# Expert stage of a four-stage block: normalisation and routing inside it, biases and closing norm batch by batch

## What is computed

```
x = layernorm(x + attention(x))              # 16 heads of 64, causal, rotary
# expert stage, 16 experts, 512 hidden, top 4
dist2  = sum((x - keys)**2, -1)
logits = -dist2 + x @ rw.T + rb              # per token 16 values
topv, topi = top_k(logits, 4); w = softmax(topv)
hidden = gelu(x @ w1[e].T + b1[e])           # all 16 experts, all tokens
out[e] = hidden @ w2[e].T + b2[e]
x = layernorm(x + sum_k w[k] * out[topi[k]])
# then 16-head attention over 4 batches, and two layers of local attention with a gated MLP
```

## Time and profile before

| | |
|---|---|
| time of three executions | median 1795.65 us (1795.16 to 1800.93) |
| the profiled execution | 1793.86 us, span 1792.0 us, mean granted PE clock 0.94 |
| PE busy | 1565.2 us, 87% of the span |
| DVE busy | 1209.4 us, 67% |
| ACT busy | 1096.4 us, 61% |
| POOL busy | 533.5 us, 30% |
| up projections, line 937 | 780 matmuls, 191.9 us |
| down projections, line 967 | 768 matmuls, 189.1 us |
| expert stage | 496.67 us to 898.19 us of the span |

### The profile page before, as it was taken

How to read it: one execution, slowest core, us unless ns; L and a number is a source line. 1 busy time by engine, 2 the same in 40 slices (tenths; PEclk the granted TensorE clock), 3 DMA queues, 4 the chain that set the end, 5 groups by cost and what they waited for, 6 DMA issues and landing times. The chain is left out here.

```text
span 1792.0 us, 31754 instructions
## 1 busy us (share of the span) xinstructions
PE 1565.2 (87%) x10386; PEld 1060.9 (59%) x10386; DVE 1209.4 (67%) x2313; ACT 1096.4 (61%) x2369; POOL 533.5 (30%) x479
## 2 busy tenths in 40 slices
PE   6999999999769999999888888858888786898875
PEld 4777777777548888888632323325555553656543
DVE  2676676676457777777666766747878646788744
ACT  2555555555258888888546666636776634767641
POOL 1222222232122222222100000027666504666621
PEclk9999999999669999999878988988999998999988
DMA  7000000000012122221000000000000000000000
GB/s 218 1 2 1 0 0 0 0 0 1 0 50 71 70 70 71 75 75 60 0 0 1 1 0 1 1 1 1 1 1 0 0 1 1 1 2 0 0 0 24
DMA packets 18812, 36.05 MB, mean 20 GB/s; under 512 B 5606, under 2 KB 10850, under 8 KB 16546
## 3 DMA queue, kind: packets, MB, share of 16 engines
q1 hardware_dynamic: 18738, 35.08, 5.8%
HBM read 33.90 MB, written 1.18 MB: 20 GB/s over the span
## 5 line engine op out<-in xcount | busy, mean ns | idle before, releaser
L873 DVE TENSOR_TENSOR m_hidp<-m_hid,m_hidp 128x512 fp32r<-128x512 f32 x260 | 182.1, 725 | 81.8 <-ACT m_hidp L832 81.6
L389 ACT ACTIVATE a_prob<-ps,a_negmax 128x512 f32<-128x512 f32 (+3 forms) x256 | 133.8, 525 | 143.8 <-DVE a_negmax L460 143.8
L837 ACT ACTIVATE m_hid<-ps,pre_w 128x512 f32<-128x512 f32 x260 | 176.9, 685 | 51.5 <-PE ps L937 51.4
L937 PE MATMUL ps<-m_xp,m_w1p 128*128 128x512 f32 x780 | 191.9, 396 | 8.1 <-DVE m_xp L865 7.2
L967 PE MATMUL ps<-m_hidp,m_w2p 128*128 128x512 f32 x768 | 189.1, 394 | 0.0
L1140 ACT ACTIVATE c_sb_pT<-ps 128x1024 f32<-128x1024 f32 x128 | 130.3, 1024 | 89.9 <-PE ps L1321 88.6
L1605 ACT ACTIVATE l_sb_prob<-ps,l_sb_negmax,l_sb_rn 128x192 f32<-128x192 f32 (+1 forms) x256 | 123.9, 494 | 92.1 <-DVE l_sb_negmax L1702 92.0
L344 POOL TENSOR_TENSOR a_qk_r<-a_qk_c,a_qk_s 128x512 f32<-128x512 f32 x64 | 81.5, 1273 | 331.0 <-DVE a_qk_s L451 331.0
L1198 DVE TENSOR_REDUCE c_sb_negmax<-ps 128x2 f32<-128x1024 f32 x128 | 153.8, 1220 | 38.7 <-PE ps L1305 38.2
L937 PEld LDWEIGHTS ps<-m_xp,m_w1p 128*128 128x128 f32 x780 | 148.8, 191 | 41.5 <-DVE m_xp L865 7.3
L967 PEld LDWEIGHTS ps<-m_hidp,m_w2p 128*128 128x128 f32 x768 | 144.1, 188 | 33.7
(11 more groups left out here) (227 smaller groups left out, 3360.9 us busy)
## 6 DMA issues: line engine op xcount, KB each, us to landing
m_gate_all<-m_gates_d SPq DMA_DIRECT2D x16, 1024.0 KB, 4.6
pre_w<-w1T SPq DMA_DIRECT2D x14, 258.0 KB, 2.7
pre_w<-w2T SPq DMA_DIRECT2D x14, 256.0 KB, 2.8
pre_wqkv<-wqkv SPq DMA_DIRECT2D x2, 768.0 KB
keep_xT<-xT SPq DMA_DIRECT2D x1, 1024.0 KB, 6.9
keep_x<-x SPq DMA_DIRECT2D x1, 1024.0 KB
out<-keep_x SPq DMA_DIRECT2D x4, 256.0 KB
pre_m_w<-l_w SPq DMA_DIRECT2D x2, 341.0 KB
```

The lines of the kernel that those rows point to most:

```text
L389: nc.scalar.activation(prob[:, u % 4, 0:width(p)], score_ps(b, p, j)[:, 0:width(p)], ACT.Exp, bias=negmax[:, u:u + 1], accum_out=den[:, b ...
L837: nc.scalar.activation(hid[:, c % 2, f, :], ps[:, f, :], ACT.Gelu, bias=w1[:, k, FF + f:FF + f + 1]).then_inc(gelu_done, 1)
L873: nc.vector.tensor_tensor(hidp[:, c % 2, 1, f, :], hid[:, c % 2, f, :], hidp[:, c % 2, 0, f, :], ALU.subtract).then_inc(low_done, 1)
L937: ins = nc.tensor.matmul(ps[:, f, :], w1p[:, k, a, f * P:(f + 1) * P], xp[:, b, c, :], start=(i == 0), stop=(i == 2))
```

## The change

- `attention0` ends with its last addition to x. Its `Norm`, the router and the logits are gone from it; keysT, rwT and rb are loaded with the later stages' constants, rb to all partitions.
- `experts0` begins with the normalisation, batch by batch. DVE takes the moments, POOL makes 1/sqrt(var + eps) and also -mean/sqrt(var + eps), ACT normalises with scale and bias, PE transposes into banks 4, 5, 6 and 4, ACT copies both to xT and to the high part xp, DVE makes the low part from PSUM. PE routes each batch with four matmuls; DVE adds the bias (a 128x16 tile, made with one matmul of ones and keys squared) when it takes the logits, and finds the maxima per batch.
- POOL's split of the first weights stands between the batches.
- The exp of the gates is issued before the GELUs of step 0. PE does up(1) before the gates' transposes, which use banks 6 and 7.
- Steps 0 to 7 and 56 to 63 are written out, the loop has 6 pairs. The b2 matmul of batch c follows the down projection of step c, its addition follows on DVE.
- No up projection, GELU or low part is made for a step 64.
- In the last expert the closing work of each batch (back transposition, copy, moments, 1/sqrt, normalising, transposition, copy) stands one to two steps behind its last gating, in the lists of all engines.

The core of the diff:

```diff
 # POOL
+        def deviation(i, b):
+            pool.wait_ge(mv_done, r + 1)
+            nc.gpsimd.tensor_tensor(var[:, i, t], mv[:, i, t, 1], eps[:, :], ALU.add).then_inc(norm_step, 1)
+            if i == 0:
+                nc.gpsimd.tensor_tensor(nmean[:, t], mv[:, 0, t, 0], neg_one[:, :], ALU.mult).then_inc(norm_step, 1)
...
+            nc.gpsimd.tensor_tensor(rstd[:, i, t], var[:, i, t], neg_half[:, :], ALU.pow).then_inc(rstd_done, 1)
+            if i == 0:
+                nc.gpsimd.tensor_tensor(nbias[:, t], nmean[:, t], rstd[:, 0, t], ALU.mult).then_inc(rstd_done, 1)
...
+        deviation(0, 0)
+        deviation(0, 1)
+        split_up(0, 0)
+        deviation(0, 2)
+        deviation(0, 3)
+        split_down(0, 0)
+        split_up(1, 1)
+        split_down(1, 1)
 # ACT
+        def normalise(b):
+            act.wait_ge(rstd_done, 2 * (b + 1))
+            for t in range(b * TPB, (b + 1) * TPB):
+                ins = nc.scalar.activation(x[:, t, :], x[:, t, :], ACT.Identity, scale=rstd[:, 0, t:t + 1],
+                                           bias=nbias[:, t:t + 1])
...
+        normalise(0)
+        normalise(1)
+        copy_xT(0)
+        normalise(2)
+        copy_xT(1)
+        normalise(3)
+        copy_xT(2)
+        copy_xT(3)
+        act.wait_ge(top_sub, 1)
+        nc.scalar.activation(tope[:, :, :], tops[:, :, :], ACT.Exp).then_inc(top_exp, 1)
         gelus(0, 0, 0)
...
+        def step(n, e, k, c, last):
+            if not (last and c == NB - 1):
+                gelus(n + 1, (c + 1) % NB, (k + (c + 1) // NB) % 2)
+            if last and c >= 1:
+                copy_x(c - 1)
+            if last and c >= 2:
+                copy_fin(c - 2)
 # DVE
+        def take_logits(b):
...
+            nc.vector.tensor_tensor(logits[:, tiles(b), :],
+                                    ps[:, b, 0:TPB * NE].rearrange("p (t e) -> p t e", e=NE),
+                                    rbias[:, None, :].broadcast_to([P, TPB, NE]), ALU.add).then_inc(lg_ev, 1)
...
+            nc.vector.tensor_tensor(xT[:, c, :], xT[:, c, :], gated[:, c % 2, :], ALU.add
+                                    ).then_inc(acc_done, 1)
+            if isinstance(n, int) and n < NB:
+
+                dve.wait_ge(b2_mm, c + 1)
+                dve.wait_ge(acc_done, NB + n + 1)
+                nc.vector.tensor_tensor(xT[:, c, :], ps[:, 6 + c % 2, :], xT[:, c, :], ALU.add).then_inc(b2_add, 1)
+            if last and c >= 2:
+                finish_norm(c - 2)
+            if last and c >= 1:
+                second_moments(c - 1)
+
+        each_step(dve, step)
+        finish_norm(NB - 2)
+        second_moments(NB - 1)
+        finish_norm(NB - 1)
 # PE
+        turn(0)
+        turn(1)
+        route(0)
+        turn(2)
+        route(1)
+        turn(3)
+        route(2)
+        route(3)
+        pe.wait_ge(w_split, 2)
+        pe.wait_ge(x_low, 1)
         up(0, 0, 0)
...
+        def step(n, e, k, c, last):
+            if not (last and c == NB - 1):
...
+                    up(n + 1, c + 1, k)
+            if at(n, 0):
+                pe.wait_ge(x_low, NB)
+                pe.wait_ge(gate_step, 7)
+                for b in range(NB):
+                    turn_gates(b)
...
+            ins.then_inc(down_mm, 1)
+            if isinstance(n, int) and n < NB:
+                bias_down(c)
+            if last and c >= 1:
+                turn_x(c - 1)
+            if last and c >= 2:
+                turn_fin(c - 2)
+
+        each_step(pe, step)
+        turn_x(NB - 1)
+        turn_fin(NB - 2)
+        turn_fin(NB - 1)
```

More of the change, by code:

```diff
@@ L274, in attention0 @@
     y_add = sem("y_add")
-    lg_mm = sem("lg_mm")
-    lg_ev = sem("lg_ev")
     NWEIGHTS = 10
-    NLATER = 5
+    NLATER = 3
     NI = NP0 * NB
     SCALE = HD0 ** -0.5
-    norm = Norm(nc, ctx, keep, ps, [0, 1, 2, 3], y_add, [NI - NB + b + 1 for b in range(NB)], "an_")
     block = ctx.enter_context(nc.Block())
@@ L522, in _ @@
         add_y(NI - 1, NB - 1)
[L525 to L532, removed]
     @block.tensor
@@ L677, in _ @@
         output(NI - 1)
[L678 to L690, removed]
 def experts0(nc, ctx, io, keep):
@@ L762, in experts0, with tiles, each_step, pair_of @@
     acc_done = sem("acc_done")
+    fin_norm = sem("fin_norm")
+    fin_mm = sem("fin_mm")
+    fin_ev = sem("fin_ev")
     STEPS = NE * NB
-    norm = Norm(nc, ctx, keep, ps, [0, 1, 2, 3], x_ev, [1, 2, 3, 4], "mn_")
+    TURN = [4, 5, 6, 4]
     block = ctx.enter_context(nc.Block())
+    def tiles(b):
+        return slice(b * TPB, (b + 1) * TPB)
+    def each_step(eng, step):
+        def pair_of(pair, last):
+            for k in range(2):
+                for c in range(NB):
+                    step(pair * (2 * NB) + (k * NB + c), pair * 2 + k, k, c, last and k == 1)
+        pair_of(0, False)
+        with eng.Fori(1, NE // 2 - 1) as pair:
+            pair_of(pair, False)
+        pair_of(NE // 2 - 1, True)
+    def at(n, k):
+        return isinstance(n, int) and n == k
     @block.sync
@@ L942, in _ @@
+        pe.wait_ge(consts, 4)
+        pe.wait_ge(route_step, 1)
+        nc.tensor.matmul(ps[:, 7, 0:NE], ones[:, :], keys_sq[:, :], start=True, stop=True
+                         ).then_inc(sq_mm, 1)
+        turn(0)
[6 more added lines that the diff above has]
+        route(3)
         pe.wait_ge(w_split, 2)
+        pe.wait_ge(x_low, 1)
         up(0, 0, 0)
-        pe.wait_ge(gate_step, 8)
-        for b in range(NB):
-            for t in range(TPB):
-                ins = nc.tensor.transpose(ps[0:NE, 4 + b, t * P:(t + 1) * P], gates[:, b * TPB + t, :], ident[:, :])
-            ins.then_inc(gT_mm, 1)
@@ L981, in _, with step @@
-        norm.tensor(pe)
+        def step(n, e, k, c, last):
+            if not (last and c == NB - 1):
+                if c == NB - 1:
+                    pe.wait_ge(w_split, 4 * (e + 1) + 2)
+                    up(n + 1, 0, 1 - k)
+                else:
+                    if at(e, 0):
+                        pe.wait_ge(x_low, c + 2)
+                    up(n + 1, c + 1, k)
+            if at(n, 0):
+                pe.wait_ge(x_low, NB)
+                pe.wait_ge(gate_step, 7)
+                for b in range(NB):
+                    turn_gates(b)
+            if c == 0:
+                pe.wait_ge(w_split, 4 * (e + 1))
+            pe.wait_ge(low_done, (n + 1) * FB + 2 * FB)
+            pe.wait_ge(mul_done, n + 1)
+            for f in range(FB):
+                for i, (a, b) in enumerate(passes):
+                    ins = nc.tensor.matmul(ps[:, 4 + c % 2, :], w2p[:, k, a, f, :], hidp[:, c % 2, b, f, :],
+                                           start=(f == 0 and i == 0), stop=(f == FB - 1 and i == 2))
+            ins.then_inc(down_mm, 1)
[5 more added lines that the diff above has]
+                turn_fin(c - 2)
```

284 lines of the change are left out of this document (179 added, 105 removed).

## The result

The changed kernel takes 1767.64 us (median of 4; 1762.30 to 1777.12), the kernel before beside it 1796.09. The profiled execution took 1764.99 us, its span is 1763.0, mean granted clock 0.949.

The account below looks back on a forecast made before the run. TensorE was taken to bound the expert loop, with gains reachable only around it: opening 23.9 less biases 3.4 gives 20.5, plus end 5.9, is 26.4 us. Forecast 1768.5 us, range 1761 to 1779.

Parts of the forecast that it names:

- The likeliest case: Whole kernel: the forecast of 1768.5 us, own range 1764 to 1774, given a chance of 0.64.
- Opening, 25.3 less 1.4 for the clock: Start of expert stage: down(0) starts 25.3 us earlier, less 1.4 for its lower clock, so 23.9 gained.
- sooner: Rival: clock stays up through turn_fin and down(0), normalising costs its lower bound; 1763 us, chance 0.08.
- Matmuls of the bias row, 8.5: Routing: 16 matmuls adding the bias row, 0.53 us each, are gone, 8.5 us in all.
- up(1) hidden, 4.2: Opening: up(1) runs on TensorE while VectorE forms the gates, so it is hidden, worth 4.2 us.
- Exp ahead of the GELUs: Opening, ScalarE: exp issued during the index search needs no table load; one load of 1.28 us leaves the path.
- Second biases, 3.4: First four loop steps: four bias matmuls cost 0.85 us each, 3.4 together, bounds 3.4 and 6.8.
- The loop body itself is the same.: Expert loop: body unchanged, so no change in its cost was reckoned beyond the second biases.
- Gate rows: First gating waits 4 us for gate rows, hidden by a hair; rival, landing 4 us later: 1772, chance 0.09.
- The end, 5.9: End of expert stage: spare up projection gone and closing work by batch save 5.9 us, bounds 4 and 8.
- only moved: Rival: batches don't overlap routing and up(1) isn't hidden, only deleted work saves, 11.5 us; 1784, chance 0.05.
- Slower loop: Rival: each up projection waits for its GELU, every one of 60 steps grows; 1805 at 0.6 us, chance 0.04.

Follow-up runs that it names:

- after_again: The changed kernel run once more, unaltered; 1768.6 us, ratio 0.9840 to the kernel before.
- i_best: Changed kernel with waiting closing transposes behind the last down projection, loop tiles at before's addresses, first w1 split behind all four batches' deviations; 1765.7 us.
- f_rank1: Changed kernel with 16 rank-1 matmuls (row of ones by row of zeros) put back into the routing; 1774.5 us, ratio 0.9851 to before.
- d_late_up: Changed kernel with up(1) put back behind the gates' transposes on TensorE; 1771.4 us, ratio 0.9856 to before.
- e_late_exp: Changed kernel with the exp put back behind the GELUs of step 0 on ScalarE; 1778.3 us, ratio 0.9867 to before.
- a_written_out: Kernel before with pairs 0 and 7 written out and nothing made for step 64; 1794.2 us, ratio 0.9984 to before.
- h_addresses: Changed kernel, same instructions, with the loop's tiles at the SBUF addresses of before; 1764.2 us, ratio 0.9802 to before.
- b_again: Repeat of a_written_out plus the second biases moved to steps 0 to 3, old opening and closing; 1789.5 us, ratio 0.9955 to before.
- c_closing_by_batch: b_again's kernel plus the closing normalisation batch by batch, so the changed kernel with before's opening; 1793.7 us.

## Why the prediction came out right

The sum was 26.4 and the stage gave 29.4 and 27.9 (S of after and after_again, against before's). The likeliest case held; its terms did less well than their sum. That the time came within 0.9 us of the forecast is partly luck: the opening gained 4.8 more than reckoned and the end 2.6 or 1.0, the biases cost 1.6 more and the loop 2.7 that were not reckoned at all.

- **Opening, 25.3 less 1.4 for the clock.** Measured 28.8, less 0.1 for a down(0) of 3.03 and not 2.94: 28.7, so 4.8 off. The steps in order: first batch ready on POOL as said (4.8 us behind the start of the last add_y, predicted 5.0); the normalising instruction 0.41 a tile for 0.37; POOL's split between the batches, which was reckoned in, held ScalarE 0.95 back, and i_best shows it was on the path. Then the routing: 0.43 a matmul and not the 0.53 read from the mixed rows, route(2) and route(3) together 3.4 and not 4.2. up(0) starts 18.4 us behind the add_y, for 20.8 predicted. The remaining error is the clock: since up(0) and up(1) run until just before the transposes, TensorE idles 0.56 us there (1.39 in after_again) and eight transposes take 1.03, all sixteen with their pause 2.4 for the 3.6 taken from before, and down(0) takes 3.03 and not 4.6. That is one half of the rival "sooner" (0.08), the clock: it stayed up in the opening in both profiles, and through turn_fin(0) and down(63) in one of them. Its other half, a cheaper normalising instruction, did not come: 0.41 is above the 0.37.
- **Matmuls of the bias row, 8.5.** f_rank1: 10.2, of which 9.1 on the path. Right in kind, mis-sized.
- **up(1) hidden, 4.2.** d_late_up: 3.7.
- **Exp ahead of the GELUs.** Counted as one load of 1.28 off the path. e_late_exp shows 5.8, some 1.0 of it by `hit`'s new place, since the whole chain behind the sum and the clock hang on it. The load itself: 1.28, and what follows starts 1.30 after its start, in after once and in e_late_exp twice. The Trainium skill (ScalarE: Activation LUTs, What ACT_TABLE_LOAD costs) gives 2.66 for a switch with its drain; no drain shows in these traces, where the same three loads start 0.01 to 0.02 behind the end of the instruction before them.
- **Second biases, 3.4.** Measured 5.0, inside the bounds (3.4 to 6.8). Halving the price with the clock was right for bias matmuls in a row: twice 0.43 in a_written_out at clock 1.00. What failed was to carry it into the loop. There the next up projection starts 1.05 behind the bias matmul's start and not 0.86, and the rounded matmuls before and after take 0.09 longer each: 1.25 a step. Weight loads that no longer hide would fit (none runs for 0.76 ahead of the next up projection's, in the PEld row above), but no run shows it.
- **"The loop body itself is the same."** The step that failed: a change of the loop's price was put at nothing. The same instructions cost 2.65 us more, by where their tiles lie (h_addresses: all of it back).
- **Gate rows.** The first gating starts 4.5 us behind the end of down(0), about as predicted (4). VectorE has no work for 1.71 of it and nobody else waits; the rival fell.
- **The end, 5.9.** Measured 8.5 and 6.9. down(63) was predicted 9.1 us behind the gating of step 61 and started 8.9 behind; it took 3.05 and 4.58 for 4.8. But the reason given for the gain was wrong in one point: b_again and c_closing_by_batch show that closing by batch lost 1.8 in E (0.6 by the profiles in which the clock held), and the spare up projection and the moved biases made all of the gain, the latter paid for in the loop.

So by S, each kernel against the one before it: no step 64 3.1 (a_written_out), biases -0.4 (b_again), closing by batch -1.8 (c_closing_by_batch), and from there to after the opening 29.2, the rest of the placement -1.9 (5.573 for 5.540, 57 steps), and the end 1.2 or -0.3, by down(63)'s clock. Sum 29.4 or 27.9, as measured. The rival "only moved" (1784) fell: the opening's overlap is real, though the biases did only move. "Slower loop" named the right place with the wrong mechanism and a tenth of the size.

## What to carry to other kernels

In a stretch where engines hand small results round, look at what is queued behind each wait: the wait of down(63) was worth 2.4 us for a change of order alone, the split in front of batch 2 1.0, and `hit` behind the sum would be worth about as much once the exp is late. Work moved from a late idle place into a loop that one engine bounds is paid there in full, and here at more than its price in a row of its own (1.25 for 0.86); test such a move by itself. When a loop's pitch changes though its body doesn't, put its tiles back at their old addresses before looking further, and read parts below the scatter of the medians as distances in the trace.

## What the runs showed of the hardware

- Placement in SBUF alone moved the step of 24 rounded 128x512 matmuls between 5.527, 5.540 and 5.573 us, each repeated to 0.001 us in the profiles of four kernels, on more than one chip. That it is placement is shown for 5.573 against 5.527 (h_addresses). The cause within the chip stays open.
- A fp32 matmul of 16x512 took 0.86 us in a row of its kind at clock 1.00 and 1.7 at 0.50; between rounded ones, at 1.00, it lengthened a step by 1.25 us.
- At clock 0.50 a routing matmul (128x16) follows its like at 0.43 us, and a pair of it and a rank-1 one takes 1.07.
- The gates' transposes behind different idle times of TensorE: after 0.44 to 1.46 us the first eight took 1.03, after 3.38 us sixteen took 3.29, after 5.73 us 3.57.
- The same idle time does not always give the same clock: behind 2.55 to 2.58 us of it twelve matmuls took 3.04 to 3.06 us in four profiles and 4.01 to 4.58 in three.
- The third stage, the same instructions in every kernel, took 298.5 us at a granted clock of 0.88 and 312.4 at 0.82.
